# A hybrid attention and feed-forward kernel: the filters' band matrices come from the host, one transfer of 6 KB rows for eight channels

## The reference, cut to what matters

```python
def _fir(x, filt):          # depthwise, causal, filt has 3, 15 or 63 taps
    b, l, h, d = x.shape
    K = filt.shape[-1]
    xf = jnp.transpose(x.reshape(b, l, h * d), (0, 2, 1))
    y = jax.lax.conv_general_dilated(xf, filt.reshape(h * d, 1, K), (1,), [(K - 1, 0)],
                                     feature_group_count=h * d)
...
local_s, local_m, local_l = _fir(v_direct, fir_s), _fir(v_direct, fir_m), _fir(v_direct, fir_l)
o = p0 * local_s + p1 * local_m + p2 * local_l + p3 * delta_out + p4 * v_direct
```

## Time and profile before

| | us |
|---|---|
| median of three runs (2459.3 to 2461.65) | 2460.59 |
| the profiled execution | 2465.9 |
| its span | 2463.3 |
| `project`, until SP may go on to the next block | 0 to 363.4 |
| `weights_fir` and the hand-over after it | 363.4 to 618.2 |
| `delta` and the loading of the feed-forward weights | 618.2 to about 1190 |
| `ffn` | about 1190 to 2463.3 |

### The profile page before, as it was taken

One profiled execution on the slowest core, in us unless ns is written; L12 is line 12 of the kernel. 1 busy time (PEld: TensorE's weight loads), 2 busy tenths in 40 slices (PEclk: granted clock), 3 DMA queues, 4 the chain that ended last, 5 costly groups with the idle time before them and its releaser, 6 DMA issues.

```text
span 2463.3 us, 40437 instructions
## 1 busy us (share of the span) xinstructions
PE 2157.7 (88%) x15412; PEld 1857.6 (75%) x15412; DVE 1235.2 (50%) x1846; ACT 905.7 (37%) x1420; POOL 576.3 (23%) x416
## 2 busy tenths in 40 slices
PE   7887865655799999944999999999999999999998
PEld 5776755555688888833888888888888888888887
DVE  5776757896556776755143323432343233323332
ACT  4454530002233333324344434443444344434442
POOL 2555555896343444310000000000000000000000
PEclk9999977887799999976999999999999999999999
DMA  3558768787877887733000000000000000000000
GB/s 128 189 197 204 198 194 202 195 210 243 223 179 177 197 206 191 170 119 124 1 18 17 0 17 17 17 0 17 17 17 0 17 17 17 0 17 17 18 1 18
DMA packets 342570, 234.45 MB, mean 95 GB/s; under 512 B 280946, under 2 KB 315250, under 8 KB 331890
## 3 DMA queue, kind: packets, MB, share of 16 engines
q1 hardware_dynamic: 334258, 232.65, 34.2%
q10 hardware_dynamic: 8256, 1.05, 0.4%
HBM read 145.31 MB, written 88.34 MB: 95 GB/s over the span
## 4 chain that ended last, share of the span: by engine, by line
PE 51%; issue 1%; DVE 1%; ACT 0%; DMA 0%; POOL 0%; DVEq 0%; SPq 0%; ACTq 0%; POOLq 0%
PE B L1611 46%; PE O L1639 5%; PE T L1569 1%; DVE yb L1738 0%; ACT gate L1677 0%; DMA x<-x_s 0%; DVE stats L1769 0%; ACT L1677 0%; DVE z L1764 0%; DVE xl L1718 0%; DVE z L1760 0%; DVE z L1783 0%; ACT xh L1665 0%; POOL rstd L1819 0%; DVEq L1733 0%
## 5 line engine op out<-in xcount | busy, mean ns | idle before, releaser
L1611 PE MATMUL B<-act1l,wr 128*128 128x512 f32 x1024 | 398.5, 389 | 0.0
L1611 PE MATMUL B<-act0h,wr 128*128 128x512 f32 x1024 | 398.3, 389 | 0.0
L1611 PE MATMUL B<-act0l,wr 128*128 128x512 f32 x1024 | 398.3, 389 | 0.0
L1611 PE MATMUL B<-act1h,wr 128*128 128x512 f32 x1024 | 398.3, 389 | 0.0
L1691 ACT ACTIVATE yb<-B,scol 128x512 f32<-128x512 f32 x256 | 176.2, 688 | 581.1 <-PE B L1611 581.1
L1726 DVE TENSOR_TENSOR act0l<-yb,act0h 128x512 fp32r<-128x512 f32 x256 | 176.1, 688 | 378.0 <-ACT act0h L1694 375.8
L1816 POOL TENSOR_TENSOR rstd<-mv,ln_eps 128x4 f32<-128x4 f32 x16 | 3.2, 199 | 1305.0 <-DVE mv L1777 1305.0
L378 DVE SCALAR_TENSOR_TENSOR acc<-proj,taps,acc 128x512 f32<-128x512 f32 x288 | 214.4, 750 | 95.2 <-ACT acc L333 86.6
L1726 DVE TENSOR_TENSOR act1l<-yb,act1h 128x512 fp32r<-128x512 f32 x128 | 88.6, 692 | 295.5 <-ACT act1h L1694 295.5
L223 PE MATMUL proj<-xt,w_qkv 128*128 128x262 f32 x768 | 195.7, 402 | 37.7 <-DMA xt<-in_xt 20.9
L1611 PEld LDWEIGHTS B<-act1h,wr 128*128 128x128 f32 x1024 | 192.3, 188 | 39.9
(11 more groups left out here) (163 smaller groups left out, 3468.6 us busy)
## 6 DMA issues: line engine op xcount, KB each, us to landing
qk_s<-yT SPq DMA_DIRECT2D x16, 1024.0 KB, 5.8
kk_s<-kfull SPq DMA_DIRECT2D x16, 1024.0 KB, 3.9
qk<-qk_s SPq DMA_DIRECT2D x16, 1024.0 KB, 5.4
lt<-kk_s SPq DMA_DIRECT2D x15, 1024.0 KB, 5.3
wraw<-in_ffn_w SPq DMA_DIRECT2D x11, 1024.0 KB, 7.3
toe<-in_firp SPq DMA_DIRECT2D x64, 160.0 KB, 3.3
xt<-in_xt SPq DMA_DIRECT2D x16, 524.0 KB, 3.9
k_s<-ktok SPq DMA_DIRECT2D x16, 512.0 KB, 3.8
```

Of the source, the lines that this page charges most:

```text
L1611: last = nc.tensor.matmul(B[slot % 4][:, :], w, part, start=(k == 0 and i == 0), stop=(k == kts - 1 and i == len(parts) - 1))
```

## The change

The host lays out the complete band matrices, zeros included, as `toe` of shape (32, 128, 8, 3, 64). The three transfers of `toeplitz(n)` become one, with 128 rows of 6144 contiguous bytes (786 KB) on both sides. POOL's two fills and SP's wait for them (`toe_zero`) go, and PE's wait for a buffer counts one transfer in place of three.

```diff
-        FIRST = [(WIN + 1 - k) // 16 * 16 for k in FIRS]
...
-        win_in, toe_in, toe_zero = st.pair("p2_win_in"), st.pair("p2_toe_in"), st.sem("p2_toe_zero")
+        win_in, toe_in = st.pair("p2_win_in"), st.pair("p2_toe_in")
...
                 def toeplitz(n):
-                    for f, k in enumerate(FIRS):
-                        src = io["firp"]
-                        sp.dma_start(toe[n % 2][FIRST[f]:, :, f, :],
-                                     bass.AP(tensor=src.tensor, offset=(n * TCH * NF + f) * FIRPAD + FIRST[f],
-                                             ap=[[1, P - FIRST[f]], [NF * FIRPAD, TCH], [1, WIN]])).then_inc(toe_in[n % 2], 16)
+                    sp.dma_start(toe[n % 2][:, :, :, :], io["toe"][n]).then_inc(toe_in[n % 2], 16)
...
-                sp.wait_ge(toe_zero, 2)
                 toeplitz(0)
...
-                        pe.wait_ge(toe_in[part % 2], (part // 2 + 1) * (16 * NF))
+                        pe.wait_ge(toe_in[part % 2], part // 2 * 16 + 16)
...
-                for i in range(2):
-                    nc.gpsimd.memset(toe[i][:, :, :, :], 0.0).then_inc(toe_zero, 1)
...
+    where = np.arange(P)[:, None] + np.arange(WIN)[None, :]
+    toe = firp[:, :, where].reshape(D // TCH, TCH, NF, P, WIN).transpose(0, 3, 1, 2, 4)
```

More of the change, by code:

```diff
@@ L1885, in host_layout @@
     const[:, C_SEL:C_SEL + 2] = i // DK == np.arange(2)[None, :]
-    return {"x": x, "xt": xt, "w_qkv": w_qkv, "w_gate": w_gate, "taps": taps, "firp": firp, "prm": prm, "ffn_w": ffn_w,
+    return {"x": x, "xt": xt, "w_qkv": w_qkv, "w_gate": w_gate, "taps": taps, "toe": toe, "prm": prm, "ffn_w": ffn_w,
             "scol": scol, "srow": g["w3_s"][None], "const": const, "w_o": kmajor(g["Wo"]),
```

## The result

The changed kernel takes 2468.4 us (median of 7, 2463.2 to 2471.7), the kernel before 2460.6 (median of 7, 2457.9 to 2462.5): 1.0033 of it, 95% interval 1.0023 to 1.0043. I had forecast 2449.7, faster, with 2443.0 to 2456.0 as the range; the change went the other way.

What follows compares the result with a forecast made beforehand. The stage was taken as bound by DVE's chain and partly by SP's transfer queue; 2.5 (start) + 1.6 (418 us) + 5.6 (head ends) + 1.2 (588 us) = 10.9 us off 2460.6 gave 2449.7, range 2443.0 to 2456.0.

Steps and rivals of the forecast that it cites:

- What bounds the stage: Stage from 363.4 to 618.2 us: DVE's chain of 64 rounds, with DVE's waits ending on transfers of SP's queue.
- The start: Stage start up to weigh(0): SP's queue starts 3.3 us earlier, weigh(0) comes sooner; 2.5 us gained, range 1.7 to 3.8.
- the rounds behind weigh(0): After the start: gains at 418 us (1.6), the ends of heads 0 and 1 (5.6) and 588 us (1.2).
- first rival: Stage start: `tri` starves beside SP's large rows, ACT's exponential is late, weigh(0) 5.8 us later, total 2458.0; chance 0.07.
- work in, work out: Stage start: with engines full until 391 us, summed transfer work sets the end, 391.5 us before, 390.3 with the change.
- The cost of a set: One set of band matrices on the DMA engines: 2.53 us before, 1.95 after (bounds 1.95 to 3.5).
- The sign that I had named: Queue view of a stretch with band matrices alone: over 350 GB/s if the forecast holds.
- The landing of w_qkv: Existing transfer with 6144-byte rows, landing 4.1 us from issue, taken as support for the lower set cost.
- The band matrices at 418 and 588 us: DVE's waits for band matrices: 1.6 us gained at 418 us, 1.2 of 4.88 at 588 us.
- The ends of the heads: Ends of heads 0 and 1, DVE waiting for the next windows: 2.8 us gained at each, 5.6 together.
- The rule of fixed time plus bytes: Band matrix transfers: fixed part plus bytes over one rate, whatever the pieces; each set would cost 0.45 us more.
- third rival: Band matrix sets no faster, only issues count: 3.0 to 4.0 us gained, about 2457; chance 0.10.

Runs made afterwards that it cites:

- a1: Changed kernel with ACT's last two `tri` transfers issued behind its exponential, square roots and scale tables: 2460.5 us, 1.0004 of the kernel before.
- a2: Changed kernel with POOL's two fills and SP's wait for them put back ahead of toeplitz(0): 2461.3 us, 1.0003 of the kernel before.
- b1: Changed kernel with the last eighth of the next head's windows issued one step earlier: 2462.2 us, 1.0011 of the kernel before.
- b2: Changed kernel with last two `tri` issues late, windows' last eighth a step earlier, POOL's triangle clearing behind round 16: 2455.0 us, 0.9985 of before.
- b3: Kernel before with last two `tri` issues late, windows' last eighth a step earlier, POOL's triangle clearing behind round 16: 2454.7 us, ratio 0.9983.
- a3: Kernel before with all 128 partitions in each of three 256-byte-piece transfers, no fills, no wait for them: 2472.8 us, ratio 1.0051.

## Why the prediction was wrong, step by step

**What bounds the stage** was right: DVE, and its waits for SP's queue. Its busy time did not move.

**How the miss divides.** I forecast 10.9 us less in this stage and the traces have 5.9 more, 16.8 apart. The start is 8.8 of it (6.3 more where I had 2.5 less) and turns the sign; the rounds behind weigh(0) are the other 8.0 (0.4 less where I had 8.4 less). The start is explained by a1 and a2; the rounds only in part.

**The start** was the step that failed, +6.3 where I had -2.5: that ACT's exponential would come no later than about 378 us, so that DVE's own chain "delays nothing". Its own first rival came true there nearly to the number: the fourth issue back 24.0 us after the stage's start (387.5 in the trace of before; measured 24.2), weigh(0) 5.8 us later (6.3). I gave it 0.07. The agreement to 0.2 us is partly luck. The rival has 1280 small rows moved by the end of the large ones and the issue back after 4900; by the records some 3130 had moved when the last window row was in, at 21.2 us, and the issue came back only after 5334. And the rival's own total, with the other 8.4 us won, was 2458.0, 10.4 under the measured one. I had the row that shows the exchange, 407 beside 410, and argued it away by the 0.7 us between SP's issues, "while few large rows are queued the small ones need not take turns". The small ones did not get through between SP's issues: `tri`'s second transfer began 10.4 us after the start. And I had written the condition down without working out when the fourth issue returns under each of the two arbitrations.

**That no instruction waits for its own transfer** was tacit in my sum: "work in, work out" conserves the engines' time, and it did: by the records the last of `tri`, head 0's windows and the first two sets was in 29.0, 29.0 and 28.7 us after the start before and 27.8, 28.1 and 27.9 with the change, about the 1.2 us less that my sum had. It does not conserve who stands behind an issue. a1, level with the kernel before (1.0004), shows that this was the loss.

**POOL's clearing** was missing. It lay under DVE's 1.8 us wait for the weights' table and came out when that wait was gone: 1.7 us at weigh(2) against the trace that I forecast from, 1.5 over the first seven rounds in the means.

**The cost of a set**: 0.5 us less from first packet to last, 0.6 less of the engines' time, and an issue a microsecond shorter. The difference was right and both values were too low: 2.53 and 1.95 forecast, 3.6 to 3.8 and 3.0 to 3.3 measured as spans. The sign that I had named, over 350 GB/s, came for the second part of a set (0.42 MB in 1.0 us) and not for a whole one (786 KB in 3.0 to 3.3 us, 240 to 260 GB/s). The landing of w_qkv, 4.1 us, which I used as support, was a single good case; the median set lands 5.1 us after its issue:

```profile
toe<-in_toe SPq DMA_DIRECT2D x32, 768.0 KB, 5.1
```

**The band matrices at 418 and 588 us**: 1.6 and 1.2 forecast, nothing and a loss of 0.6 measured. At 418 the interval varies from 2.3 to 4.0 us between executions of the same kernel, more than the term, so nothing can be read there. At 588 it is 6.1 to 6.7 us before and 6.4 to 7.5 with the change; why the shorter sets win nothing there is not shown.

**The ends of the heads**: 2.8 forecast, 2.5 measured at the first and 0.8 at the second. What is waited for was right (b1), the size at the second was not: the interval there is 6.8 to 7.4 us in the kernel before and 5.7 to 6.9 in the changed one. (The terms that I listed, 1.0 + 0.4 + 0.6 + 0.6, make 2.6 and not the 2.7 that I wrote or the 2.8 that I took.) Why the second gives so much less than the first I have not shown.

**The rule of fixed time plus bytes.** The prediction took it from the Trainium skill ("DMA: Bandwidth & Descriptors", Anatomy of one DMA), where the fit is for transfers that GpSimd issues; those of this stage are issued by SP and ACT. By it a set would cost an estimated 0.45 us more; the sets' spans are 0.5 us less, so the traces do not bear it out here. My third rival, sets no faster and only the issues shorter, would have given about 2457 and no starvation; that b2 and b3 come out level is near what it says of the rounds, but the sets did become faster, and what uses up their gain is open.

**What would have shown it.** I had named the fourth `tri` issue and 378 us, 14.5 after the stage's start, as the sign of the first rival; it returned 24.2 us after it. Other signs came true in the first trace and proved nothing: DVE's waits for filter groups fell to 13.8 us, under the 15 that I had named, and to 5.1 at the end of head 0, while waits for ACT and POOL took their place.

## What to carry to other kernels

A transfer's issue can hold the engine that issues it until an earlier transfer has moved, so compute queued behind issues on ScalarE is on the path of the transfers: put the small work first (issuing from SyncE instead was not tried here). When a change lets one queue start sooner or with longer rows, ask what the other queue's small rows will get, since in the stretches where both were full the two took turns packet by packet and not byte by byte. And where an engine waits at the end of a phase for the last part of the next phase's data, issue that part a step earlier before making anything ahead of it faster: one window transfer of each head, moved up a step, was worth 5 to 6 us here, the new data layout nothing that could be measured.

## What the runs showed of the hardware

- Two queues on the same engines, both full, exchanged packets one for one, 128 bytes against mostly 4096: 268 beside 268 in 4 us, 409 beside 409 in the next, and 59/59, 47/47, 48/48, 60/59 in single half microseconds.
- The first row of a set of eight 6 KB rows on each engine took 0.23 to 0.95 us in the mean of the 16 engines, 0.53 in the median set; the median of the others was 0.234.
- How long an issue on ACT's queue held ACT went with how fast the rows issued before it moved: 19.75 us for two issues of 2048 rows each in the changed kernel, 4.72 before, 6.56 in a2, 10.50 in a3. By the records the fourth issue came back when 4900 to 5800 of the 8192 rows had passed, in all ten traces in which I counted, whether that was 7 or 25 us after the start.
- Windows to 64 partitions moved at 225 GB/s and to 128 at 404, and again at 0.89 MB and 1.48 MB in 4 us (222 and 370 GB/s, beside `tri`'s rows) in the changed kernel.
